# The band mask of the score strips: from the VectorE reduction to small accumulating matmuls

## The reference, cut to what matters

```python
x = x + 0.5 * ffn(layernorm(x))       # top-2 routed experts; an expert over its capacity is dropped whole
x = x + attention(layernorm(x))
x = x + 0.5 * ffn(layernorm(x))

# attention: B=4, T=2048, D=256, 16 heads of 16
dist = abs(idx[:, None] - idx[None, :])
attend = (dist <= 128) | glb[:, None] | glb[None, :]      # position 0 attends and is attended everywhere
logits = where(attend, q @ k.T * 0.25, -inf)
out = softmax(logits) @ v @ Wo.T
```

## Time and profile before

| what | value |
|---|---|
| median of 3 runs | 870.89 us (870.79 to 871.8) |
| profiled execution, first to last instruction | 867.2 us |
| PE matmul busy | 814.6 us (94%), 21504 matmuls |
| PE weight loads busy | 606.9 us (70%) |
| DVE busy | 758.3 us (87%) |
| ACT busy | 637.2 us (73%) |
| POOL busy | 488.1 us (56%) |
| mean granted TensorE clock | 0.997 |

### The profile page before, as it was taken

One profiled execution on the slowest core, in us unless ns is written; L12 is line 12 of the kernel. 1 busy time (PEld: TensorE's weight loads), 2 busy tenths in 40 slices (PEclk: granted clock), 3 DMA queues, 4 the chain that ended last, 5 costly groups with the idle time before them and its releaser, 6 DMA issues. The chain is left out here.

```text
span 867.2 us, 50607 instructions
## 1 busy us (share of the span) xinstructions
PE 814.6 (94%) x21504; PEld 606.9 (70%) x21505; DVE 758.3 (87%) x2819; ACT 637.2 (73%) x1417; POOL 488.1 (56%) x874
## 2 busy tenths in 40 slices
PE   9798999999999999999999999898999999999894
PEld 8555667767777777667778777666778777766572
DVE  7898899989887899998987899998988889998785
ACT  2268888897877667998877666898777766888850
POOL 3212556675555557765554465675554556656763
PEclk9999999999999999999999999999999999999998
DMA  7722224432212344441213335352222335220113
GB/s 231 116 81 75 67 73 121 135 88 70 77 62 96 111 146 119 120 127 62 89 51 101 106 105 161 108 131 71 74 73 68 106 93 149 94 77 18 49 51 102
DMA packets 93191, 83.51 MB, mean 96 GB/s; under 512 B 17568, under 2 KB 92192, under 8 KB 92960
## 3 DMA queue, kind: packets, MB, share of 16 engines
q1 hardware_dynamic: 91360, 78.91, 30.1%
q10 hardware_dynamic: 1600, 1.31, 1.0%
HBM read 20.66 MB, written 8.39 MB: 33 GB/s over the span
## 5 line engine op out<-in xcount | busy, mean ns | idle before, releaser
L1105 ACT ACTIVATE probs<-bank 128x384 f32<-128x384 f32 (+1 forms) x1024 | 462.8, 480 | 146.8 <-PE bank L962 137.4
L1431 DVE CUSTOM_DVE_ANT_0 bank<-bank,con 128x288 f32<-128x288 f32 x1024 | 494.4, 518 | 53.2 <-PE bank L934 44.8
L934 PE MATMUL bank<-k_stack,q_stack 96*32 96x288 bf16 x4096 | 325.4, 288 | 10.7 <-DVE row_max L1431 5.7
L962 PE MATMUL bank<-q_stack,k_stack 99*32 99x288 bf16 (+2 forms) x4096 | 319.8, 285 | 16.0 <-ACT probs L1105 9.7
L980 PE MATMUL bank<-probs,v_sb 128*32 128x128 f32 x5888 | 305.4, 272 | 3.6 <-issue 1.5
L1218 POOL TENSOR_SCALAR_AFFINE_SELECT probs<-probs 128x512 f32<-128x512 f32 x240 | 154.8, 645 | 180.1 <-ACT probs L1105 179.5
L980 PEld LDWEIGHTS bank<-probs,v_sb 128*32 128x32 f32 x5888 | 192.1, 110 | 36.7 <-issue 5.3
L962 PEld LDWEIGHTS bank<-q_stack,k_stack 99*32 99x32 bf16 x4096 | 123.6, 95 | 79.7 <-ACT probs L1105 53.5
L934 PEld LDWEIGHTS bank<-k_stack,q_stack 96*32 96x32 bf16 x4096 | 127.3, 95 | 74.0 <-DVE row_max L1431 21.3
L1223 POOL TENSOR_SCALAR_AFFINE_SELECT probs<-probs 128x512 f32<-128x512 f32 x240 | 154.1, 642 | 19.3 <-ACT probs L1105 19.2
L823 PE MATMUL bank<-xnT,wqk_sb 128*32 128x256 f32 x2048 | 158.1, 379 | 0.6 <-DVE neg_max L1453 0.5
(11 more groups left out here) (126 smaller groups left out, 737.2 us busy)
## 6 DMA issues: line engine op xcount, KB each, us to landing
q_stack<-pieces SPq DMA_DIRECT2D x384, 64.0 KB, 2.7
k_stack<-pieces SPq DMA_DIRECT2D x364, 64.0 KB, 2.7
x_ring<-in_x SPq DMA_DIRECT2D x28, 512.0 KB, 4.5
out_x<-x_ring SPq DMA_DIRECT2D x16, 512.0 KB, 3.9
attn<-in_x SPq DMA_DIRECT2D x4, 512.0 KB, 6.0
wback_sb<-in_wback SPq DMA_DIRECT2D x8, 256.0 KB, 6.0
k_stack<-pieces ACTq DMA_DIRECT2D x20, 64.0 KB, 3.6
q_stack<-neg_max SPq DMA_DIRECT2D x48, 16.0 KB, 2.3
```

What stands on the lines that cost most here:

```text
L934: last = pe.matmul(a_ring[i % len(a_ring)][SP * s:SP * (s + 1), 0:WIN], q_stack[g % 2][0:KROWS, h, q:q + SP], k_stack[g % 2][0:KROWS, h, q ...
L962: last = pe.matmul(b_ring[i % len(b_ring)][SP * s:SP * (s + 1), start:final], k_stack[g % 2][0:SROWS, h, WINDOW + P * j + SP * s:WINDOW + ...
L1105: act.activation(probs[:, j % 4, h, c0:c1], b_ring[i % len(b_ring)][:, c0:c1], ACT.Exp, scale=LOGIT_SCALE).then_inc(S["exp_ready"], 1)
L1431: dve.tensor_tensor_reduce(out=a_ring[i % len(a_ring)][:, 0:WIN], in0=a_ring[i % len(a_ring)][:, 0:WIN], in1=mask, scale=1.0, scalar=con[: ...
```

## The change

The strip gets its mask on PE. After the four matmuls of a strip PE multiplies a bf16 identity (32 of its columns at a time) with a bf16 copy of the mask and accumulates into the strip, for those columns only that can be outside: 64 columns (the two edges, one matmul per 32 rows) in tiles 1 to 14, 128 + 32 columns (two matmuls per 32 rows) in tiles 0 and 15. VectorE then takes a plain maximum (`tensor_reduce`) of the bank. `a_ring` has two banks instead of three, `b_ring` three instead of two. ScalarE makes the bf16 copies of the identity and of the three masks once at the start, ahead of its wait for `pads_ready`; the mask load gets a semaphore of its own, and `setup_in` counts four loads.

```diff
-        a_ring, b_ring, o_bank, misc = banks[0:3], banks[3:5], banks[5], banks[6:8]
+        a_ring, b_ring, o_bank, misc = banks[0:2], banks[2:5], banks[5], banks[6:8]
...
+        def both_edges(strip):
+
+            return strip.rearrange("p (b c) -> p b c", c=SP)[:, 0:2 * WINDOW // SP + 1:2 * WINDOW // SP, :]
...
+        def mask_parts(t):
+
+
+            if t == 0:
+                return lower_half, upper_edge
+            if t == NT - 1:
+                return lower_edge, upper_half
+            return both_edges,
...
+                        sp.dma_start(con[:, C_BAND:C_PICK], consts[:, C_BAND:C_PICK]).then_inc(S["band_in"], 16)
                         for dst, src in (
-                                (con[:, C_BAND:C_PICK], consts[:, C_BAND:C_PICK]),
...
                             if first and n == 0 and h == 0:
                                 pe.wait_ge(S["pads_ready"], 1)
+                                pe.wait_ge(S["masks_ready"], 2)
...
                             for s in range(4):
                                 q = P * t + SP * s
-                                last = pe.matmul(a_ring[i % len(a_ring)][SP * s:SP * (s + 1), 0:WIN],
-                                                 q_stack[g % 2][0:KROWS, h, q:q + SP],
-                                                 k_stack[g % 2][0:KROWS, h, q:q + WIN],
-                                                 start=True, stop=True)
+                                pe.matmul(a_ring[i % len(a_ring)][SP * s:SP * (s + 1), 0:WIN],
+                                          q_stack[g % 2][0:KROWS, h, q:q + SP],
+                                          k_stack[g % 2][0:KROWS, h, q:q + WIN],
+                                          start=True, stop=False)
+                            for parts in mask_parts(t):
+                                for s in range(4):
+                                    strip = a_ring[i % len(a_ring)][SP * s:SP * (s + 1), 0:WIN]
+                                    last = pe.matmul(parts(strip), ident_half[:, SP * s:SP * (s + 1)],
+                                                     parts(band_half[:, mask_of(t), :]),
+                                                     start=False, stop=parts is mask_parts(t)[-1])
                             last.then_inc(S["a_full"], 1)
...
+                        act.wait_ge(S["ident_in"], 16)
+                        act.activation(ident_half[:, :], ident, ACT.Copy).then_inc(S["masks_ready"], 1)
+                        act.wait_ge(S["band_in"], 16)
+                        act.activation(band_half[:, :, :], band_all, ACT.Copy).then_inc(S["masks_ready"], 1)
                         act.wait_ge(S["pads_ready"], 1)
...
-                            if first and n == 0 and h == 0:
-                                dve.wait_ge(S["setup_in"], 16 * 5)
...
-                            dve.tensor_tensor_reduce(
-                                out=a_ring[i % len(a_ring)][:, 0:WIN], in0=a_ring[i % len(a_ring)][:, 0:WIN], in1=mask,
-                                scale=1.0, scalar=con[:, C_LOWEST:C_LOWEST + 1], op0=ALU.add,
-                                op1=ALU.max, accum_out=row_max[:, g % 2, h, t:t + 1]).then_inc(S["a_free"], 1)
+                            dve.tensor_reduce(row_max[:, g % 2, h, t:t + 1], a_ring[i % len(a_ring)][:, 0:WIN],
+                                              AX.X, ALU.max).then_inc(S["a_free"], 1)
```

More of the change, by code:

```diff
@@ L79, in build @@
         ones = sb("ones", [P, P])
+        ident_half = sb("ident_half", [P, P], BF16)
+        band_half = sb("band_half", [P, 3, WIN], BF16)
         neg_half = sb("neg_half", [P, 4])
@@ L121, in build @@
         take = ident.rearrange("p (h c) -> p h c", c=SP)[:, :, 0:VW]
-        band = [con[:, C_BAND + i * WIN:C_BAND + (i + 1) * WIN] for i in range(3)]
+        band_all = con[:, C_BAND:C_BAND + 3 * WIN].rearrange("p (i c) -> p i c", i=3)
         pick = con[:, C_PICK:C_PICK + NG * SP].rearrange("p (g c) -> p g c", g=NG)
@@ L130, in build @@
         banks = [ctx.enter_context(nc.psum_tensor(f"bank{i}", [P, 512], FP32)) for i in range(8)]
-        a_ring, b_ring, o_bank, misc = banks[0:3], banks[3:5], banks[5], banks[6:8]
+        a_ring, b_ring, o_bank, misc = banks[0:2], banks[2:5], banks[5], banks[6:8]
         names = ["setup_in", "ident_in", "wqk_in", "pick_in", "ones_ready", "wo_in", "half_ready", "x_first0", "x_first1", "x_first2", "x_first3", "x_ring0", "x_ring1", "x_ring2",
-                 "wqk_ready", "pads_ready", "k_ones", "v_pads", "wback_in",
+                 "wqk_ready", "band_in", "masks_ready", "pads_ready", "k_ones", "v_pads", "wback_in",
                  "stats_ready", "moments_ready", "eps_added", "rstd_ready", "shift_ready", "xn_ready",
@@ L367, in pv_count, with mask_of, lower_half, lower_edge @@
             return g * (3 * NT - 2) + min(3 * i + part, 3 * NT - 2)
+        def mask_of(t):
+            return 0 if t == 0 else 2 if t == NT - 1 else 1
+        def both_edges(strip):
+            return strip.rearrange("p (b c) -> p b c", c=SP)[:, 0:2 * WINDOW // SP + 1:2 * WINDOW // SP, :]
+        def lower_half(strip):
+            return strip[:, 0:WINDOW]
+        def lower_edge(strip):
+            return strip[:, 0:SP]
+        def upper_half(strip):
+            return strip[:, WIN - WINDOW:WIN]
+        def upper_edge(strip):
+            return strip[:, WIN - SP:WIN]
+        def mask_parts(t):
[4 more added lines that the diff above has]
+            return both_edges,
         def window(j):
@@ L832, in _ @@
                                 if first and b == 0 and t == 0:
-                                    pe.wait_ge(S["setup_in"], 16 * 5)
+                                    pe.wait_ge(S["setup_in"], 16 * 4)
                                 pe.wait_ge(*emptied("XT", early_index[b, t // 4], t % 4 // 2))
@@ L1422, in _ @@
                             g, t = divmod(n, NT)
-                            mask = band[0 if t == 0 else 2 if t == NT - 1 else 1]
                             i = HG * n + h
-                            if first and n == 0 and h == 0:
-                                dve.wait_ge(S["setup_in"], 16 * 5)
                             if h == 0 and t == 0 and g >= 2:
```

## The result

| | before | after |
|---|---|---|
| median | 871.35 us (870.79 to 873.92) | 922.56 us (918.35 to 927.42) |
| profiled execution, first to last instruction | 867.2 us | 915.5 us |
| PE busy, matmuls | 814.6 us, 21504 | 844.5 us, 26112 |
| DVE busy | 758.3 us | 700.5 us |

The ratio is 1.0584, 95% interval 1.0533 to 1.0634: slower by 5.8%. The prediction had the sign right and the size wrong, +6.8 us for +48.3 us of span; 922.56 us lies beyond the upper end of its range, 891 us.

What follows compares the result with a forecast made beforehand. PE was taken to bound the full stretches, VectorE the opening, and DVE, ACT and PE in turn the mixed ones. 17.8 - 7 - 1 - 3 = +6.8 us of span gave 877.7 us, eight-in-ten range 858 to 891.

Steps and rivals of the forecast that it cites:

- full stretches: Three stretches, 394 us together, where PE is almost never idle: +17.8 us (15 to 24).
- mixed ones: Stretches, 338 us together, where DVE, ACT and PE hold each other up in turn: net -7 us (-22 to +8).
- opening: 27 to 64 us, VectorE-bound: -1 us (-4 to +2), as the ring of two takes most of the quicker maximum's gain.
- after the last maximum: Tail from 796 us: -3 us (-4.5 to 0), as three B banks spare exponentials the wait for scores.
- mask group: A strip's added mask matmuls on PE: 30 ns for a group of four with 64 columns.
- rivals 4: PE: a mask group costs 66 ns, +18 us in full stretches and 4 more in mixed, 899 us; chance 0.05.
- 5: PE: matmul starts never under 25 ns apart, +36 us in the full stretches alone, 914 us; chance 0.01.
- VectorE's step: Plain maximum takes 0.45 us, next step at 0.37 us: 0.07 us saved a strip, 34 us in mixed stretches.
- The ring of two: Two A banks let PE run only one quarter ahead: +2 us in the full stretches (0 to 8).
- Rival 3: Two-bank A ring eats the gain, PE waiting for every second maximum in VectorE bursts: +20 us, 891 us; chance 0.09.
- The masks: Mask matmuls on PE, priced by columns: 37 ns a mean strip, 17.8 us for 480 strips, in full and mixed alike.
- The ScalarE copies: Two start-up copies ahead of ScalarE's first real work at 11.90 us, after 9.59 us of idling: put at nothing.

Runs made afterwards that it cites:

- e3_nomask_a3b2: Kernel after with three A banks, two B banks and no mask matmuls, so a plain maximum over all 288 columns: 867.89 us, ratio 0.994.
- e4_nomask_a2b3: Kernel after without the mask matmuls, keeping its two A banks and three B banks: 882.27 us, ratio 1.0113 to the kernel before.
- e1_mask_a3b2: Kernel after, masks on PE, but with three A banks and two B banks as before: 933.77 us, ratio 1.0696 to the kernel before.
- e11_mask_less_dma: e1_mask_a3b2 with a quarter of the bytes in each stack DMA from the third group on: 914.56 us, ratio 1.0467.
- e5_wide_mask_a3b2: e1_mask_a3b2 with each mask part as one matmul over all 128 rows instead of four over 32: 1076.95 us, ratio 1.2312.

## Why the prediction was wrong

In the prediction's own terms: full stretches +17.8 us forecast, +27.0 measured; mixed ones -7 and +21.1; opening -1 and +3.5; after the last maximum -3 and -3.4. The mixed stretches are 28 of the 41.5 us by which the sum was off.

**The mask group, right.** PE's matmuls in order of time in the kernel after, near 259 us:

```profile
259.38 0.30 PE L970 MATMUL bank<-k_stack,q_stack 96*32 96x288 bf16 x4
259.50 0.20 PE L977 MATMUL bank<-band_half,ident_half 128*32 128x64 bf16 x4
259.53 0.39 PE L1022 MATMUL bank<-probs,v_sb 128*32 128x128 f32 x8
259.75 0.30 PE L1004 MATMUL bank<-q_stack,k_stack 99*32 99x288 bf16 x4
```

The next group starts 0.03 us after the mask group, as forecast (30 ns), and that is also the median of the whole trace. That also drops rivals 4 (66 ns) and 5 (25 ns for each matmul, 100 ns a group): a matmul of such a group takes 8 ns in the mean.

**VectorE's step, right, its worth overrated.** One group of the page, and one place of VectorE's order of time:

```profile
L1473 DVE TENSOR_REDUCE row_max<-bank 128x1 f32<-128x288 f32 x1024 | 447.1, 452 | 140.9 <-PE bank L977 127.1
```

```profile
202.40 0.81 DVE L1473 TENSOR_REDUCE row_max<-bank 128x1 f32<-128x288 f32 x2
```

0.45 us each, 0.36 us for the second of a pair (forecast 0.45 and 0.37). But 76 us less busy time of VectorE (758.3 us to 682.1 in `e3_nomask_a3b2`) made the kernel 4.8 us shorter, 5.1 us in the mixed stretches. This is the step that failed first: I let 25 of PE's 45 us of waits there go, for the relief and the third B bank together, and reasoned from the 91% that VectorE was busy. In place of -25 us the two together measured -5.1 + 7.7 = +2.6 us. The waits for exponentials that the third bank removes are real (53.5 us to 5.9), but the kernel gains nothing by it, since PE then stands before the A ring: in the mixed stretches the exchange of a bank is +7.7 us. As no run has three banks on both sides, it stays open whether the removed waits would have come back at the A ring even with its three banks.

**The ring of two, underrated.** I had +2 us for it in the full stretches (0 to 8), and it measured +6.5; nothing of its own in the mixed ones, +7.7; and the opening was to gain 1 us and lost 2.0 us by it. Rival 3 named this mechanism with +22 us in the full stretches and a time of 891 us. The mechanism is there, with 13.3 us in all; the rest of the time beyond it is the masks'. Its 891 us still falls 31.6 us short of the 922.56. (Rivals 4 and 5 have times nearer to it, 899 and 914 us, by a price of the mask group that the rows above refute.) Its price depends on how long the bank is read: 31 us by the times with the old maximum, 14 us with the new.

**The masks, right in columns, blind to instructions.** In the full stretches they measured +20.3 us for 17.8 predicted: 4.3 us of stops at block boundaries and 16.0 us of the rest. In the mixed ones I had 17.8 us too, and +18.5 measured looks like a hit, but it is luck: 11.8 us of it are such stops, which no term had, and only 6.7 us the rest. Of the 39.8 us over the span 25.4 - 9.5 = 15.9 us are stops without a wait (9.5 us being those of `e4_nomask_a2b3`), and 23.9 us the rest, 23 ns a strip instead of 37. With three A banks it is 67.6 us: 58.3 - 14.6 = 43.7 us of stops and again 23.9 us. No step of the prediction asked how many instructions PE runs in a microsecond, though the page before had the instruction queue on it and the earlier trace rows the counts: from 43600 PE instructions in 867 us to 52816 in 915, from 4.8 us for 256 to 4.2 us in the first full stretch. The time of the stops is the term that it put at nothing. The two errors hide each other: with the ring of two fewer blocks are quick (12 under 3.25 us against 18) and PE runs dry less often, 25.4 us of stops in the kernel after against 58.3 in `e1_mask_a3b2`.

**Opening and tail.** After the last maximum -3.4 us (forecast -3): exponentials in a backlog come 0.38 us apart, 8 in 3.17 us, forecast 0.40. The opening is 3.5 us longer instead of 1 us shorter, 2.0 of it the ring's. The granted clock there was 0.96 in the kernel after and in `e4_nomask_a2b3`, and 1.00 before; what part of the 3.5 us that is, no run tells. The ScalarE copies were nearly free, ACT in order of time in the kernel after:

```profile
10.35 0.92 ACT L1055 ACTIVATE band_half<-con 128x864 bf16<-128x864 f32 x1 [5.14 <-DMA con<-in_consts]
11.94 0.60 ACT L1083 ACTIVATE xnT<-bank 128x512 f32<-128x512 f32 x1 [0.67 <-PE bank L794]
```

11.94 us for 11.90 us before, with 0.67 us to spare, not the several that an idle ScalarE suggested.

**The marks that the prediction set.** Full stretches 15 to 20 us longer: 27. PE busy over 99% in them: 97%. Waits for exponentials about 30 us: 5.9. Waits for maxima not down: up, to 57.5 us. Of these the 97% is the plainest sign that something not in the sum had entered: an engine that bounds a stretch, gets more work, and is then less busy.

**A version a little ahead of both.** `e3_nomask_a3b2`, plain maximum, three A banks, no mask in pass one: 867.89 us, 0.6% below before (0.3 to 0.9%). Pass one only needs a value near the row's largest score, as pass two's cut removes the columns outside the window; with these inputs the maximum over all 288 columns serves. It would not if a score outside stood so far above those inside that their exponentials vanish.

## What to carry to other kernels

Where an engine issues many short instructions, count them per microsecond as well as their columns: here PE stopped at nearly every 256th instruction when the last 256 had taken under 3.25 us, and hardly ever above 4.5 us, and a change that adds cheap instructions pays there. Before a bank is moved from one ring to another, read who waits longest on either side with the new occupancy, as here 49 us fewer waits on one side came with 72 us more on the other. Test the parts of a change apart: the plain maximum gained, and the two parts that came with it to pay for the mask lost eleven times as much.

## What the runs showed of the hardware

- PE's instructions come in 16 KB packets of 256, which start no closer than 3.1 us; in the kernel after a stop ends 1.2 to 1.6 us after the end of its packet. The stops appear in the waits as "issue".
- Data DMAs add to these stops: 33 MB less of them took 58.3 us of stops to 39.6 us (`e1_mask_a3b2`, `e11_mask_less_dma`).
- The packet for the next block starts in the median 1.26 us after PE crossed the last boundary and takes 1.22 us, and the next boundary is crossed no sooner than 1.2 us after it (`e1_mask_a3b2`).
- A 128-row-wide matmul between groups of 32-wide ones costs about 0.2 us a strip, its 64 columns included (`e5_wide_mask_a3b2`).
- Matmuls of a single column with their weight loads cost 11 to 12 ns each by the times (23 us for 2048, 49 us for 4096), with the stops in it.
